# A shared batch moved behind the expert tiles, one batch of gathers moved into the attention, and a longer ring of up weights in the first layer

## The reference, cut to what matters

```python
x = x + L0_attn(layernorm(x))   # linear recurrence over time and an MLP
x = x + L0_ffn(layernorm(x))    # 8 experts, 2 per token, gelu(t @ w1[e].T) @ w2[e].T, weighted
x = x + L1_attn(layernorm(x))   # causal attention, 16 heads of 8
x = x + L1_ffn(layernorm(x))    # 8 experts, 2 per token, and a shared MLP:
# shared = gelu(xf @ sw_up + sb_up) @ sw_down + sb_down; out = shared + combined experts
# out = out / (max(abs(out), axis=-1) + 1e-6)
```

## Time and profile before

| what | us |
|---|---|
| median of the three runs | 972.75 |
| the profiled execution | 970.3 |
| its span | 968.5 |
| layer 0 tiles, PE busy in 158.3 to 252.5 | 84.56 of 94.20 |
| attention's steady part, PE busy in 293.0 to 661.5 (mean granted clock 0.99) | 351.75 of 368.50 |
| shared batches 0 to 3, PE busy in 704.9 to 750.6 | 42.13 of 45.70 |
| layer 1 tiles, PE busy in 755.1 to 910.2 | 153.28 of 155.10 |
| shared batches 4 to 7, PE busy in 910.2 to 954.2 | 40.39 of 44.00 |
| after the last matmul, 954.2 to 968.5 | 14.30, DVE busy 10.99 |

### The profile page before, as it was taken

One profiled execution on the slowest core, in us unless ns is written; L12 is line 12 of the kernel. 1 busy time (PEld: TensorE's weight loads), 2 busy tenths in 40 slices (PEclk: granted clock), 3 DMA queues, 4 the chain that ended last, 5 costly groups with the idle time before them and its releaser, 6 DMA issues. The chain is left out here.

```text
span 968.5 us, 18634 instructions
## 1 busy us (share of the span) xinstructions
PE 808.7 (83%) x5585; PEld 603.0 (62%) x5585; DVE 613.9 (63%) x1402; ACT 521.3 (54%) x1092; POOL 422.9 (44%) x524
## 2 busy tenths in 40 slices
PE   2798825898559899999999999986388899999993
PEld 2566615888425556565555565546256899999762
DVE  5478653557438977877777777733811665678457
ACT  3466466665315576767767666764131466565520
POOL 2655467727578013242333332224467700273174
PEclk9899866999759999999999999995589999999997
DMA  5930013555253121212131221000012322232222
GB/s 147 366 103 1 23 46 120 158 144 139 65 171 123 39 94 39 98 33 99 43 101 65 65 97 42 26 1 0 28 44 74 106 66 76 81 114 77 77 66 65
DMA packets 82157, 80.45 MB, mean 83 GB/s; under 512 B 9858, under 2 KB 61760, under 8 KB 82112
## 3 DMA queue, kind: packets, MB, share of 16 engines
q1 hardware_dynamic: 73122, 62.68, 20.9%
q0 software_dynamic: 8192, 16.79, 5.7%
q10 hardware_dynamic: 796, 0.42, 0.2%
HBM read 41.06 MB, written 38.80 MB: 82 GB/s over the span
## 5 line engine op out<-in xcount | busy, mean ns | idle before, releaser
L1661 ACT ACTIVATE Pb<-ps,low 128x512 f32<-128x512 f32 x320 | 216.7, 689 | 134.4 <-PE ps L1760 87.6
L931 POOL DMA_INDIRECT YG<-yslots,slot x128 | 132.1, 1032 | 152.1 <-DMA yslots<-yb 82.0
L1539 DVE TENSOR_REDUCE m<-ps 128x4 f32<-128x1024 f32 x128 | 156.2, 1221 | 55.1 <-PE ps L1737 36.0
L1760 PE MATMUL ps<-Q,KZ 128*128 128x128 f32 (+3 forms) x512 | 172.1, 397 | 5.0 <-ACT Pb L1661 4.0
L390 POOL DMA_INDIRECT xslots<-XN,slot x128 | 124.7, 974 | 69.9 <-issue 37.6
L1471 POOL TENSOR_SCALAR_AFFINE_SELECT Pb<-Pb 128x512 f32<-128x512 f32 (+1 forms) x84 | 67.7, 806 | 190.0 <-ACT Pb L1661 189.3
L1760 PEld LDWEIGHTS ps<-Q,KZ 128*128 128x128 f32 x512 | 93.0, 192 | 81.8 <-ACT Pb L1661 56.1
L1313 PE MATMUL ps<-xT,wst 128*128 128x128 f32 x960 | 136.5, 280 | 7.4 <-DVE wst L1182 4.6
L1325 PE MATMUL ps<-wst,hb 128*128 128x128 f32 x960 | 134.0, 276 | 6.6 <-ACT hb L1132 6.1
L1135 ACT ACTIVATE hb<-ps,upb 128x128 f32<-128x128 f32 x320 | 91.6, 369 | 75.0 <-PE ps L1313 74.9
L1313 PEld LDWEIGHTS ps<-xT,wst 128*128 128x128 f32 x960 | 122.6, 196 | 9.1 <-DVE wst L1182 5.8
(11 more groups left out here) (258 smaller groups left out, 1240.3 us busy)
## 6 DMA issues: line engine op xcount, KB each, us to landing
xt<-xslots SPq DMA_DIRECT2D x40, 256.0 KB
yslots<-yb SPq DMA_DIRECT2D x40, 256.0 KB, 2.3
terms<-high SPq DMA_DIRECT2D x32, 256.0 KB, 2.1
Q<-terms SPq DMA_DIRECT2D x128, 48.0 KB
KZ<-terms SPq DMA_DIRECT2D x128, 48.0 KB
xslots<-YG SPq DMA_DIRECT2D x2, 2560.0 KB, 11.8
terms<-low SPq DMA_DIRECT2D x16, 256.0 KB, 2.3
X<-in_L_attn_x_dram SPq DMA_DIRECT2D x4, 512.0 KB, 5.7
```

The costliest lines, as they stand in the source:

```text
L931: pool.indirect_dma_start(out=s.YG[:, TB * w + j, k, :], out_offset=None, in_=s.yslots[group][:, :], in_offset=bass.IndirectOffsetOnAxis(a ...
L1539: w = dve.tensor_reduce(top[:, :, (TB + 1, 3, TB, None, 1)[u]], ps.rearrange("p (t g k) -> p g t k", t=2, g=HG), AX.XY, ALU.max)
L1661: act.activation(Pb[:, NCH * (gg % 2) + c, :], bank(4 + c % 2), ACT.Exp, bias=s.low[:, :], scale=DH ** -0.5)\
L1760: w = pe.matmul(ps[:, col:col + T - kt * P], KZ[:, HG * gg + g, kt * P:kt * P + P], Q2[gg % 2][:, kt * P:T], start=True, stop=not masked)
```

## The change

It makes three edits. First, `GD` in `experts` becomes 3 instead of 4: three shared batches before the tiles and five after. Second, the gathers of batch 3 in layer 0 leave the expert block and stand in attention's POOL list just after `spread(0, None)`. Third, in layer 0 the up weights get eight buffers instead of four, the extra four being views of `nb`. The first copies (tiles 0 to 7) wait for nothing. A copy is issued ten tiles ahead. Its wait on `hid_ready` becomes one for the tile eight places before. Layer 1 keeps four buffers.

```diff
-LOOSE = 3
+LOOSE, SHARED_FIRST = 3, 3
...
-    GD = GROUPS[0]
+    GD = SHARED_FIRST
...
-    up, down = s.wst[0:RING], s.wst[RING:2 * RING]
+    up, down, AHEAD = s.wup, s.wdn, len(s.wup)
...
-                for b in range(FIRST[g], FIRST[g] + GROUPS[g]):
+                for b in range(FIRST[g], FIRST[g] + GROUPS[g] - (layer == 0)):
                     gather(pool, s, sums, b)
...
             def copy_up(i, t, e):
 
-                dve.wait_ge(hid_ready, BT * i + (t + 1))
-                dve.tensor_copy(up[t % RING][:, :], W1[:, bass.ds(e, 1), :].rearrange("p e f -> p (e f)")).then_inc(up_ready, 1)
+                if not isinstance(i, int) or BT * i + t >= AHEAD:
+                    dve.wait_ge(hid_ready, BT * i + (t + 1 + RING - AHEAD))
+                dve.tensor_copy(up[t % AHEAD][:, :], W1[:, bass.ds(e, 1), :].rearrange("p e f -> p (e f)")).then_inc(up_ready, 1)
...
-            UPS = RING + 2
+            UPS = AHEAD + 2
...
-                of_tile = numbers(dve, BT * i + RING, BT + 2 if more else RING)
+                low = RING if layer else AHEAD
+                left = BT + UPS - low if not isinstance(i, int) else min(BT + UPS - low, SLOTS - BT * i - low)
+                of_tile = numbers(dve, BT * i + low, left) if left > 0 else ()
...
-                    if t + UPS < BT or more:
-                        copy_up(i, t + UPS, of_tile[t + UPS - RING])
+                    if t + UPS < low + left:
+                        copy_up(i, t + UPS, of_tile[t + UPS - low])
...
-                for t in range(RING):
+                for t in range(AHEAD):
                     copy_up(0, t, of_tile[t])
...
-                for t in range(RING, UPS):
+                for t in range(AHEAD, UPS):
                     copy_up(0, t, of_tile[t])
...
-                    m = pe.matmul(psH[t % RING][:, c * P:c * P + P], up[t % RING][:, c * P:c * P + P],
+                    m = pe.matmul(psH[t % RING][:, c * P:c * P + P], up[t % AHEAD][:, c * P:c * P + P],
...
             spread(0, None)
+            gather(pool, s, s.sums, FIRST[1] - 1)
             for r in range(2):
                 pool.wait_ge(s.stored[r], 16 * BODIES)
             for b in range(FIRST[1], B):
...
-                s.wst = [fs(f"wst{layer}{k}", [P, NC * P]) for k in range(2 * TB)]
+                s.wup, s.wdn = ([fs(f"w{n}{layer}{k}", [P, NC * P]) for k in range(count)]
+                                for n, count in (("up", 4), ("dn", 4)))
+                if layer == 0:
+                    s.wup += [s.nb[k // 2][:, 2 * (k % 2):2 * (k % 2) + 2, :].rearrange("p j d -> p (j d)") for k in range(4)]
```

## The result

The changed kernel took 956.71 us (median of 4 runs, 953.58 to 962.50) against 972.48 for the kernel before on the same chip: ratio 0.9861, 95% interval 0.9824 to 0.9898, some 13.5 us faster. The forecast was 962.4 with a range of 955.5 to 969.5.

The account below looks back on a forecast made before the run. PE, busy 83% of the span, bounds the kernel; only its waits in layer 0's tiles and the end can be won. Terms -5.49 and -3.66 sum to -9.15 us, giving 961.15 to 963.6, middle 962.4; range 955.5 to 969.5.

Parts of the forecast that it names:

- What bounds the kernel, edit 1: Only PE's idle time can be won; three front batches leave one combine after the last SH copy, -5.49 us.
- rival 3: Front: rows for layer 1's first tiles arrive over 2.9 us later, PE idles; at 8.4 us 966.6 remains; chance 0.04.
- rival 2: Kernel's end: the last combine waits for late gathers, only 3.66 us is won, 966.6 to 969.1 us; chance 0.08.
- Edit 3: Layer 0's tiles: eight up buffers remove three PE stalls after combines, -3.66 us, and the block ends that much earlier.
- rival 1: Layer 0's tiles: the wait moves to `xT`, first two stalls stay, gain 6.95 us, 963.35 to 965.8; chance 0.12.
- Edit 2: Batch 3's gathers, expert block to attention: counted 0 beyond edit 3, at most 2.2 us; attention cost 0, 14.8 us cover.
- The slower rival: Attention: gathers beside combines fall behind and DVE waits 22.6 us at the last combine, 985.0 us; chance 0.04.
- rival 4: Attention: all 40 gathers slow as the one of 1.94 us, last combine waits 22.6 us, 985.0 us; chance 0.04.
- The clock: Low-clock stretch at attention's start: PE's clock shifts favourably, taken as 4 us, giving 957.3 to 959.8; chance 0.10.
- The chances: Whole kernel: faster by over 1% 0.44, within 1% 0.51, slower by over 1% 0.05; 1% is 9.7 us.

Follow-up runs that it names:

- the version that beats both: Changed kernel with layer 1's gate copies ahead of the SH copy, two output buffers, half of each tail combine ahead of that copy: 944.46 us, ratio 0.9744 to before.
- the two late gathers: Changed kernel with two of batch 3's gathers issued behind the last DVE copy of layer 0's tiles: attention started 6.27 us behind them; profile only.

## Why the prediction was right or wrong

**What bounds the kernel, edit 1: right.** Front -10.9 and -11.2 in two of the three profiles against -10.9 forecast, tail +5.5 and +5.4, layer 1's tiles +0.6 and +0.7 where I had 0. That makes -4.8 and -5.1 for -5.49, and edit 1 alone measured -3.7 (-5.7 to -1.7). In the first profile, with the long drop, the same three stages sum to +1.5 us: the term is right only where the clock stays up. The cover in the front, which rival 3 denied, was there: the transposes waited for the SH copy in every profile. The gathers were in time at the end, with no wait before the last combine, so rival 2 did not come.

**Edit 3: right in its place, wrong in its condition.** All three stalls went. `xT` did not take their place, so rival 1 did not come. The tiles became 4.0 to 4.9 us shorter for 3.66, part of it at the body boundaries. But the sentence that turned this into time, that the attention starts 4.6 us behind the last DVE copy "whatever that copy's time", was false. Alone, the edit gave 1.0 us (-0.9 to 2.7).

**Edit 2: the step that failed.** The prediction put it at 0 beyond edit 3 and bounded it by 2.2 us. It compared the end of POOL's last issue, 250.86, with PE's end, and took the landing of 2.0 us as all that could follow. But POOL's drain, and with it the block's end, came 6.4 us behind that issue (257.26). On the kernel before, this put POOL last already, by 3.7 us over SP's drain. On one with edit 3 it would have been last by 9.71 - 0.88 = 8.8 us. The lines of the earlier trace rows held both numbers, 250.86 and 257.61, and I read 4.6 us from the copy as a constant of the block's end because the copy was the later of the two. The drains of L1033 in the trace of the kernel before would have told which it was. The term should have been -3.7 for edit 2, with edit 3's -3.66 standing only on top of it. The sum is then -12.9 us instead of -9.15, and from the median of before that gives 959.9. Of the signs that the prediction named, this one failed: from the last DVE copy to the attention's first instruction there were 0.87 us and not 4.6. That the time still fell into the range is partly luck. The low end, 955.5, came from the spread of the runs and from the clock, and nothing in it stood for this step; a later execution of the changed kernel took 953.74, below it.

**The slower rival did not come.** Eight more gathers in the attention made nothing late. The rule that rival 4 names from the Trainium skill, page "SBUF — State Buffer", section "Who interferes with whom", that VectorE and GpSimd lock a shared port pair, cost nothing on the path here: the longest gather in the attention took 1.28 us in the changed kernel's first profile, where before had one of 1.94. (The same section narrows the rule, for a VectorE instruction with two inputs in SBUF like the combine's multiply, to GpSimd instructions that read SBUF. The prediction left that out, and no run here tells whether it covers a gather.)

**The clock: a rival that partly happened.** Attention and route took 1.3 to 2.0 us less in the changed kernel. In windows of 1 us the low stretch that reaches into the first attention batch ended 25, 25 and 29 us behind the block's start in the three profiles of the changed kernel, and 34 us before. In the other kernels it ended anywhere from 25 to 38 us. This answers the earlier trace rows, for the changed kernel in a window of the same length:

```profile
249.70:285.10 35.40, 18.28 (x52) 9.17 (x52) 15.18 (x25) 5.85 (x8) 24.87 (x33) 0.71 0.42 131
```

The mean clock is 0.71 for 0.56. That the shorter stage comes from this is argued from the profiles and not isolated. With 2 us off for the attention the expected time is about 958, and the runs of the changed kernel, 953.58 to 962.50, lie on both sides of it.

**The chances.** The sum stood at 9.15 us, just inside 1%, and the result is outside it. With -12.9 us it would have been outside from the start.

## What to carry to other kernels

In this kernel a block ends when its slowest queue has drained. POOL's, with an indirect DMA as its last instruction, drained some 6 us behind the end of that DMA's issue, so look at the drains of each queue before calling a gap fixed. A gain ahead of such an end is worth nothing until the last queue is moved too: 1.0 (edit 3) and 3.9 us (edit 2) alone became 11.2 together. Before crediting a stage with a difference, profile the same kernel twice, for one drop of PE's clock moved a stage by 6 us.

## What the runs showed of the hardware that I had not expected

- The next block's first POOL instruction started 6.76 us behind the end of POOL's last gather issue in the four kernels with 32 gathers in the block, 6.43 with 28 and 6.27 with 26, of which two stood alone. POOL's drain ended 5.9 to 6.5 us behind that issue in these, and 5.8 in the changed kernel's first profile, where it held nothing up. The Trainium skill, page "Perfetto Trace Analysis", section "DMA Instruction — SWDGE (GPSIMD)", says that the shown end of such a DMA is the end of writing its descriptors (the orders to the DMA engines) and not of the transfer. The traces agree that more follows: a combine that waited for its gathers started 243.28 - 241.19 = 2.1 us behind the last issue in the changed kernel, and 1.6 in the version that beats both. So the transfer doesn't fill the 6 us, as the idle DMA engines behind the two late gathers show too. What the rest is stays open.
- All twelve profiles show a drop of PE's clock to 1.2 GHz near the change from the shared batches to layer 1's tiles. It lasted 3 to 7 us in ten of them and 20 in two, with PE busy for 17.35 of the 20 us in one.
